# Last layer of a graph network: attention columns inside the weight, denominators inverted on 128 partitions, fusion product in pairs, store in two parts

## What is computed

```python
def gat_conv(x, src, dst, W, att_src, att_dst, bias):   # W: 512 x 4 heads x 64
    h = jnp.einsum('nd,dhc->nhc', x, W)
    a_s = jnp.sum(h * att_src, axis=-1)
    a_d = jnp.sum(h * att_dst, axis=-1)
    e = jax.nn.leaky_relu(a_s[src] + a_d[dst], NEG_SLOPE)
    m = jax.ops.segment_max(e, dst, num_segments=N)
    ex = jnp.exp(e - m[dst])
    denom = jax.ops.segment_sum(ex, dst, num_segments=N)
    alpha = ex / (denom[dst] + 1e-16)
    out = jax.ops.segment_sum(alpha[:, :, None] * h[src], dst, num_segments=N)
    return out.reshape(N, HEADS * C_HEAD) + bias
fwd = gat_conv(x, src, dst, W_f, ...); bwd = gat_conv(x, dst, src, W_b, ...)
fused = jnp.concatenate([fwd, bwd], axis=1) @ W_fuse + b_fuse
mean = jnp.mean(fused, axis=0); var = jnp.mean(jnp.square(fused - mean), axis=0)
out = x + relu((fused - mean) * rsqrt(var + BN_EPS) * bn_gamma + bn_beta)
```

## Time and profile before

| | us |
|---|---|
| median of 3 runs (lowest, highest) | 1034.76 (1033.79, 1034.81) |
| the profiled execution, its own time | 1035.34 |
| its span in the trace | 1033.5 |
| TensorE busy in the span | 882.6 (85%) |
| VectorE busy | 680.3 (66%) |
| POOL busy | 517.6 (50%) |
| ScalarE busy | 454.1 (44%) |
| share of TensorE in the chain that ended last | 61% |

### The profile page before, as it was taken

One profiled execution on the slowest core, in us unless ns is written; L12 is line 12 of the kernel. 1 busy time (PEld: TensorE's weight loads), 2 busy tenths in 40 slices (PEclk: granted clock), 3 DMA queues, 4 the chain that ended last, 5 costly groups with the idle time before them and its releaser, 6 DMA issues.

```text
span 1033.5 us, 18423 instructions
## 1 busy us (share of the span) xinstructions
PE 882.6 (85%) x6852; PEld 767.0 (74%) x6852; DVE 680.3 (66%) x1310; ACT 454.1 (44%) x762; POOL 517.6 (50%) x595
## 2 busy tenths in 40 slices
PE   0789984793899989999989999989999989987785
PEld 0589863672798878798878798878899878854455
DVE  8759957569527677527668437667437578668874
ACT  1277713421347623437523447523347432355652
POOL 6147736124474237674247674246673257356741
PEclk9999998897999999999999999999999999799888
DMA  4000001011430002330002430002330012000001
GB/s 107 22 1 0 0 1 51 11 44 32 101 107 18 1 21 63 103 112 12 1 21 66 115 109 11 1 22 75 110 105 1 1 34 59 11 1 1 0 1 50
DMA packets 45752, 41.32 MB, mean 40 GB/s; under 512 B 4193, under 2 KB 34083, under 8 KB 45690
## 3 DMA queue, kind: packets, MB, share of 16 engines
q1 hardware_dynamic: 43514, 37.19, 12.5%
q10 hardware_dynamic: 2176, 3.32, 1.5%
HBM read 39.08 MB, written 1.28 MB: 39 GB/s over the span
## 4 chain that ended last, share of the span: by engine, by line
PE 61%; DVE 18%; ACT 6%; issue 6%; POOL 4%; DVEq 2%; DMA 1%; SPq 1%; POOLq 0%; ACTq 0%
PE psum L1365 23%; PE psum L1359 16%; PE psum L1457 9%; PE psum L1383 5%; PE psum L730 3%; DVE arena L1767 2%; ACT arena L1243 2%; DVE stats L1911 2%; POOL ringw L1135 1%; PE psum L1408 1%; PE psum L753 1%; DVEq L2005 1%; PE psum L642 1%; DVE hot_dst L2000 1%; DVE x L2103 1%
## 5 line engine op out<-in xcount | busy, mean ns | idle before, releaser
L1365 PE MATMUL psum<-ringw,arena 128*128 128x512 f32 (+2 forms) x558 | 127.5, 387 | 15.5 <-POOL ringw L1135 7.5
L1365 PEld LDWEIGHTS psum<-ringw,arena 128*128 128x128 f32 x558 | 101.4, 213 | 38.0 <-issue 9.1
L1070 POOL TENSOR_SCALAR acc<-acc,rden,flag 128x640 f32<-128x640 f32 x80 | 70.2, 879 | 110.9 <-DVE rden L1763 110.4
L1457 PE MATMUL psum<-ringw,arena 128*128 128x512 f32 x480 | 118.7, 396 | 3.1 <-DVE arena L1775 2.5
L1383 PE MATMUL psum<-ident,acc 128*128 128x128 f32 x560 | 82.5, 280 | 36.3 <-DVE acc L1685 32.3
L1359 PE MATMUL psum<-arena,ringw 128*128 128x320 f32 x768 | 113.3, 309 | 0.0
L1359 PEld LDWEIGHTS psum<-arena,ringw 128*128 128x128 f32 x768 | 112.9, 188 | 0.3
L1135 POOL TENSOR_TENSOR ringw<-raw,ringw 128x512 fp32r<-128x512 f32 x62 | 80.6, 1308 | 56.8 <-ACT ringw L1279 56.8
L1359 PE MATMUL psum<-arena 128*128 128x320 f32 x510 | 95.1, 327 | 14.0 <-issue 7.7
L1457 PEld LDWEIGHTS psum<-ringw,arena 128*128 128x128 f32 x480 | 87.8, 188 | 23.2 <-DVE arena L1775 3.5
L1365 PE MATMUL psum<-arena 128*128 128x256 f32 (+3 forms) x615 | 103.5, 318 | 0.0
(11 more groups left out here) (264 smaller groups left out, 1883.3 us busy)
## 6 DMA issues: line engine op xcount, KB each, us to landing
raw<-in_L_gnn_m_w SPq DMA_DIRECT2D x16, 256.0 KB
xn<-in_L_gnn_m_w SPq DMA_DIRECT2D x16, 256.0 KB
raw<-in_L_gnn_wv SPq DMA_DIRECT2D x8, 256.0 KB
xn<-in_L_gnn_wv SPq DMA_DIRECT2D x8, 256.0 KB
raw<-in_L_gnn_wq SPq DMA_DIRECT2D x8, 256.0 KB
xn<-in_L_gnn_wq SPq DMA_DIRECT2D x8, 256.0 KB
raw<-in_L_gnn_wk SPq DMA_DIRECT2D x8, 256.0 KB
xn<-in_L_gnn_wk SPq DMA_DIRECT2D x8, 256.0 KB
```

The lines of the kernel that those rows point to most:

```text
L1070: g.tensor_scalar(pbuf[:, k % 4, :], pbuf[:, k % 4, :], rden[:, k:k + 1], flag[:, 1, k % NT:k % NT + 1], ALU.mult, ALU.mult).then_inc(pn_u ...
L1365: ins = pe.matmul(to, l, r, start=(i == 0), stop=(i == len(terms) - 1))
L1457: ins = pe.matmul(brow(ROWBLK[f"{name}{t}"]), l, r, start=(pieces[0] + i == 0), stop=(pieces[-1] == KT - 1 and i == len(terms) - 1))
```

## The change

- **Start.** The 16 attention columns join the weight of the b product (`wb`, 272 columns); `own_terms` and `hidden("b", t)` become `hidden_and_own(t)`. VectorE copies the 16 columns tile by tile. All five mask turns and the f product come after three `maxima`, the target rows of the first pair after them.
- **Banks.** A maxima row lies in `source_pair` (banks of `big[1]`, for the second head `big[2]`), branch rows in `target_pair` (`big[0]`, `big[2]` in turn).
- **Order in the turns.** For an even place i the next head's second and first branch stand ahead of the head's first product, for an odd one behind its second, after the target rows. ScalarE's copies move to match.
- **Denominators.** ScalarE copies one row of each. For the first three pairs SP stores it to DRAM, loads it as 128 partitions of 2 x 5, VectorE inverts that, SP stores and loads it back, spread to 64 rows a head. The seventh head is inverted by itself on 64 partitions, the eighth as 128 partitions x 320 columns (`last_sums`).
- **Fusion product.** The first two pairs of column blocks 0 and 1 are multiplied in the last turn, the rest pair by pair. Moments are taken from PSUM; the bias enters the norm's terms.
- **End.** Blocks 0 and 1 are turned, added and stored (256 columns of all tiles), then blocks 2 and 3.
- `DVE_ADDS` has six tiles instead of four.

```diff
-DVE_ADDS = [30, 33, 36, 39]
+DVE_ADDS = [26, 28, 31, 33, 36, 38]
...
+        wide_w = L3H * L3C + 2 * NJ
+        wb = arena2[:, 0:2 * KT * wide_w].rearrange("p (s k c) -> p s k c", s=2, k=KT)
+        AT2 = 2 * KT * wide_w
...
+        den_d = nc.dram_tensor("den_d", [3, 2, NP], F32, kind="Internal").ap()
+        rec_d = nc.dram_tensor("rec_d", [3, 2, NP], F32, kind="Internal").ap()
...
+        def source_pair(i):
+            return big[2 if i == 1 else 1][:, :, 0:HALF]
+
+        def target_pair(i):
+            return big[i % 2 * 2][:, :, 0:HALF]
...
+                    g.wait_ge(share_ld[p], 32)
+                    g.tensor_tensor(comb[:, PAIR[p], :], comb[:, PAIR[p], :], denom[p], ALU.mult).then_inc(comb_up, 1)
...
+                if d == "b":
+                    act.wait_ge(acol_up, t + 1)
...
+                if i == 4 or i == 6:
+                    act.wait_ge(comb_up, p - 1)
+                rows = L3C if i == 6 else 1
+                to = mine if i == 6 else other
...
+                    act.activation(denom[p][to:to + rows, at], pacc[h][other:other + rows, 0:ROW_SPLIT[h]], ACT.Identity,
+                                   bias=tiny[other:other + rows, 0:1]).then_inc(p_read, 1)
...
+            def last_sums():
+
+                act.wait_ge(pa_full, NJ)
+                act.activation(last[L3C:P, :], pacc[0][0:L3C, 0:HALF], ACT.Identity, bias=tiny[0:L3C, 0:1]).then_inc(last_up, 1)
+                act.activation(last[0:L3C, 0:ROW_SPLIT[0] - HALF], pacc[0][0:L3C, HALF:ROW_SPLIT[0]], ACT.Identity,
+                               bias=tiny[0:L3C, 0:1]).then_inc(last_up, 1)
+                act.wait_ge(pb_full, NJ)
+                act.activation(last[0:L3C, ROW_SPLIT[0] - HALF:HALF], pacc[1][0:L3C, 0:ROW_SPLIT[1]], ACT.Identity,
+                               bias=tiny[0:L3C, 0:1]).then_inc(last_up, 1)
+                act.wait_ge(last_rec, 1)
+                act.activation(last_moved[L3C:P, :], last[0:L3C, :], ACT.Copy).then_inc(last_up, 1)
...
-                if st == 1 and i % 2 and i + 1 < NJ:
-                    target_rows((i + 1) // 2)
-                if st == 2 and i + 1 < NJ:
+                if st == 1 and i + 1 < NJ:
+                    if i % 2:
+                        target_rows((i + 1) // 2)
+                    else:
+                        second_branch(i + 1)
+                if st == 2 and i % 2 and i + 1 < NJ:
                     second_branch(i + 1)
-                if st == NT - 1 and i in (4, 6):
-                    comb_high((i - 4) // 2)
+                if st == 0 and i in (5, 7):
+                    comb_high((i - 5) // 2)
+            last_sums()
             comb_high(2)
...
+            def hidden_and_own(t):
+                u = ROW3[f"Hb{t}"]
+                if t < NROW:
+                    free_row(pe, u)
+                else:
+                    pe.wait_ge(h_read, t - NROW + 1)
...
+                row_mm(pe, brow(u)[:, 0:wide_w],
+                       sum([parts(tile_of(yT, k, t), [wb[:, s, k, :] for s in range(2)]) for k in range(KT)], [])).then_inc(h_full, 1)
...
+                if i >= 2:
+                    pe.wait_ge(main_read, MAIN[f"am{max(i - 1, 0) if i > 2 else 0}"] + 1)
...
+                pe.wait_ge(misc_read, MISC[f"vb{i}"] + 1)
...
+            for i in range(EARLY):
+                maxima(i)
             pe.wait_ge(m3_up, NT)
-            mask_turned(0)
-            mask_turned(1)
-            hidden("f", 0)
+            for t in range(NT):
+                mask_turned(t)
+                hidden(t)
             target_rows(0)
-            hidden("f", 1)
             second_branch(0)
             first_branch(0)
...
+                if st == 0 and i % 2 == 0 and i + 1 < NJ:
+                    second_branch(i + 1)
+                    first_branch(i + 1)
...
+                if st == 1 and i % 2 and i + 1 < NJ:
                     target_rows((i + 1) // 2)
-                if st == 1 and i + 1 < NJ:
...
+                    first_branch(i + 1)
+                if st == 2 and i + 4 < NJ:
+                    maxima(i + 4)
+                if n == (NJ - 1) * NT:
+                    fuse(0, range(2))
+                if n == (NJ - 1) * NT + 2:
+                    pe.wait_ge(main_read, MAIN["va6"] + 1)
+                    fuse(1, range(2))
+
+            pe.wait_ge(main_read, len(MAIN))
+            fuse(2, range(2))
+            for o in range(3):
+                fuse(o, range(2, 3))
+            for o in range(3):
                 fuse(o, range(3, 4)).then_inc(f_full, 1)
...
+                dve.reciprocal(dcol[p % 2], dcol[p % 2]).then_inc(rec_up, 1)
...
+            six = comb[0:L3C, PAIR[3], :]
+            dve.wait_ge(p_read, 4 * (NJ - 1))
+            dve.reciprocal(denom[3][0:L3C, :], denom[3][0:L3C, :]).then_inc(rec_up, 1)
+            dve.wait_ge(rec_up, 4)
+            dve.tensor_tensor(six, six, denom[3][0:L3C, :], ALU.mult).then_inc(combd_up, 1)
+            dve.wait_ge(share_ld[2], 32)
+            dve.tensor_tensor(comb[:, PAIR[2], :], comb[:, PAIR[2], :], denom[2], ALU.mult).then_inc(combd_up, 1)
+            dve.wait_ge(last_up, 3)
+            dve.reciprocal(last, last).then_inc(last_rec, 1)
+            dve.wait_ge(last_rec, 1)
+            seven = comb[L3C:P, PAIR[3], :]
+            dve.tensor_tensor(seven[:, 0:HALF], pacc[0][L3C:P, 0:HALF], last[L3C:P, :], ALU.mult).then_inc(combd_up, 1)
+            dve.wait_ge(last_up, 4)
+            cut = ROW_SPLIT[0] - HALF
+            dve.tensor_tensor(seven[:, HALF:ROW_SPLIT[0]], pacc[0][L3C:P, HALF:ROW_SPLIT[0]], last_moved[L3C:P, 0:cut], ALU.mult).then_inc(combd_up, 1)
+            dve.tensor_tensor(seven[:, ROW_SPLIT[0]:NP], pacc[1][L3C:P, 0:ROW_SPLIT[1]], last_moved[L3C:P, cut:HALF], ALU.mult).then_inc(combd_up, 1)
             comb_rest(2)
...
+                dve.wait_ge(f_full, o + 1)
+                for i, n in enumerate((HALF, N - HALF)):
+                    dve.bn_stats(bn3[:, o, i, :], fsum[o][:, i, 0:n]).then_inc(bn_up, 1)
...
+            for p in range(3):
+                sp.wait_ge(p_read, 8 * (p + 1))
+                for h in range(2):
+                    other = (1 - TURN[2 * p + h] % 2) * L3C
+                    sp.dma_start(den_d[p, h:h + 1, :], denom[p][other:other + 1, :]).then_inc(den_st[p], 16)
+                sp.wait_ge(den_st[p], 32)
+                sp.dma_start(dcol[p % 2], den_d[p].rearrange("h (q f) -> q h f", q=P)).then_inc(dcol_ld[p], 16)
+                sp.wait_ge(rec_up, p + 1)
+                sp.dma_start(rec_d[p].rearrange("h (q f) -> q h f", q=P), dcol[p % 2]).then_inc(rec_st[p], 16)
+                sp.wait_ge(rec_st[p], 16)
+                for h in range(2):
+                    mine = TURN[2 * p + h] % 2 * L3C
+                    sp.dma_start(denom[p][mine:mine + L3C, :], rec_d[p, h, :].partition_broadcast(L3C)).then_inc(share_ld[p], 16)
+            sp.wait_ge(y_up, 3)
+            store(sp, 0, 2 * P, False)
+            store(sp, 0, 2 * P, True)
+            sp.wait_ge(y_up, 6)
+            store(sp, 2 * P, 4 * P, False)
+            sp.wait_ge(y_up, 7)
+            store(sp, 2 * P, 4 * P, True)
```

More of the change, by code:

```diff
@@ L102 @@
 MAIN = {n: i for i, n in enumerate(MAIN)}
-MISC = ["mt0", "mt1", "vt0", "vb0", "mt2", "mt3", "mt4"]
+MISC = [f"mt{t}" for t in range(NT)] + ["vt0", "vb0"]
 for _i in range(NJ - 1):
@@ L893, in dve_l3 @@
                     inverse((i - 3) // 2)
[L894 removed]
+                if st == 2 and i in (5, 7):
                     comb_rest((i - 5) // 2)
```

332 lines of the change are left out of this document (155 added, 177 removed).

## The result

The changed kernel takes 1045.8 us (median of 8 runs, 1042.76 to 1047.95), the kernel before on the same chips 1036.75 us (1033.79 to 1040.95): a ratio of 1.0084, 95% interval 1.0062 to 1.0107. It is slower, by about 9 us. The median of before is here 2.0 us above the 1034.76 us that the forecast started from. The profiled execution of the changed kernel takes 1047.22 us, its span is 1045.4 us.

The account below looks back on a forecast made before the run. The prediction took a chain of hand-offs, then TensorE's own order, to bound the turns. Its terms, 0 - 1.0 + 11.4 - 3.15 - 1.4 = +5.9 us, took 1034.76 to 1040.7 us; range 1025 to 1046, own range 1037 to 1044.

Parts of the forecast that it names:

- Start, 0 forecast: Layer start through turn 0: the lead from merged matmuls is spent again, 0 us; -4.3 with the clock kept.
- The fall forecast for this place: Start, at TensorE's wait for the third head's maxima: lower clock for 5 us of work, 2.5 us more.
- Turns without falls, 77.3 forecast: Turns 1 to 7, bound by TensorE's own order, sum to 77.3 us with no fall of the clock.
- Falls, +11.4 forecast: Turns 1 to 6: six falls to the lower clock, mean 1.9 us each, +11.4 us.
- upper bound of 12.6: Turns 1 to 6: most the clock falls were to cost, 6 x 2.1 us; the lower bound was 0.
- turns -1.0: Seven turns: 77.3 us without falls against the old 78.25 us containing three falls, -1.0 us.
- Fusion, -3.15 forecast: From last value product to fusion product's end: 19.1 us becomes 15.95, -3.15 us.
- Rest, -1.4 forecast: Behind the fusion product: moments from PSUM and shorter adds save 1.4 of 11.80 us, between 0 and -3.
- Detour, 0 forecast: Denominators of three pairs through DRAM: transfers covered by the turns, costing nothing.
- the 6.6 us per transfer of the rival: Late denominators' detour: pair 2 delays the last head's chain some 4.2 us, 1044.9 us; chance 0.07.
- the clock stays up: Rival for start and turns: no falls, start -4.3 and falls 0, giving 1025.0 us; chance 0.30.

Follow-up runs that it names:

- e10_start: The changed kernel with the third head's maxima row moved behind the second pair of mask turn and f product at the start: ratio 1.0037 to the kernel before.
- e4_fuses: The changed kernel with the first two pairs' fusion pieces moved from the last turn to behind the last value product: ratio 1.0034 to the kernel before.
- e11_detour2: `e6_all` with the denominators' load of spread sums and store of inverses each made twice in a row: ratio 0.9873 to the kernel before.
- e7_wide: The changed kernel with 2 x 2 overwritten full-width products ahead of the second-branch row of even turns: ratio 0.9991 to the kernel before, turns 83.12 us.
- e6_all: The changed kernel with TensorE's former branch-row order mostly restored and early fusion pieces behind the last product: ratio 0.9883 to the kernel before.
- e8_all_wide: `e6_all` with one overwritten full-width product ahead of the first product of every turn but the last: ratio 0.9848 to the kernel before.

## Why the prediction was right, and where its steps were off

The direction and the mechanism held: 1040.7 forecast from a median of 1034.76, so +5.9 us, against +9 on the same chips. That 1045.8 lies just within the range of 1025 to 1046 is partly luck: it is above the forecast's own 1037 to 1044, and the kernel before was itself 2.0 us slower on these chips.

- **Start, 0 forecast, -1.95 measured, -0.9 by the forecast's own cuts.** Counted from the layer's start, 5.1 us later in this run, the first maximum (893.88) lies at 888.8 and the first product (920.83) at 915.7, where 889 and 916 stood. The wait for the third maxima row was 3.72 us against 3.73:

```profile
897.74 0.89 PE L683 MATMUL psum<-arena 16*128 16x320 f32 x2 [3.72 <-DVE edge_col L849]
```

  The fall forecast for this place came. From the first product to the end of turn 0 it took 7.7 us, where I had 8.3; that and the 0.3 us at the first product are the -0.9. What I missed is that this wait could be avoided by order alone (`e10_start`: -5.0).
- **Turns without falls, 77.3 forecast.** From turns at the full clock: odd 11.17 and 11.48 us (mean 11.33), even 10.63, turn 7 11.56. 3 x 11.33 + 3 x 10.63 + 11.56 = 77.4 us. That the sum agrees to 0.1 us is partly luck: the even turns are 1.2 us longer than worked out, the odd ones 0.8 us and turn 7 0.3 us shorter. The waits themselves were right: 2.7 to 3.0 us in even turns, two of 0.8 us in odd ones.
- **Falls, +11.4 forecast.** 89.97 - 77.4 = 12.5 us, at the upper bound of 12.6. There were six, but in turns 1 to 4, 6 and 7, none in turn 5. The size was off both ways: about 2.0 to 3.2 us for the four long ones, 1.5 us for the two short, where I had 1.9 for all. My mean held 1.6 us for the short fall in turn 7 of the kernel before, and that one cost its turn nothing that shows: 9.78 us, against 9.90 in turn 6 without a fall. TensorE waits 1.30 us for an exponential later in it (to 1000.19), which can hide the slower products.
- **The term "turns -1.0"** was right as a sum and hid the main thing. It set 77.3 us without falls against 78.25 with three. Turns 3 and 5 of the kernel before, at 14.29 and 13.35 us, are 7.6 us longer than two of 10.04. That was what the removed reciprocals could bring. The new order then spent it: turns at the full clock went from 9.9 and 10.04 to 10.63 and 11.33, some 6 us, and the pieces in turn 7 took 2.1 us more and 3.6 with a fall (11.56 and 13.05 against 9.48 without them). I asked whether the reciprocals were worth anything, and pointed to turns 1 and 2, which had none; the turns that had them were the ones to look at. That their removal is what freed turns 3 and 5 is read from the two waits that go back to them; no run removes them alone.
- **Fusion, -3.15 forecast, -2.14 measured.** The third pair's matmuls start 5.4 us after the last product, as worked out (5.55). The sixty matmuls were to take 10.4 us and took 11.46 (1024.09 to 1035.55), since the clock stood at its lower level until 1029.5, 5.4 us of these matmuls; in the kernel before it was 2.9 us (to 1014.3). With 36 matmuls in that wait it did not fall there (`e4_fuses`).
- **Rest, -1.4 forecast, -1.94 measured**, within its bounds.
- **Detour, 0 forecast.** The landing of the spread inverses took 3.2 us:

```profile
z<-rec_d SPq DMA_DIRECT2D x4, 160.0 KB, 3.2
```

  so the 6.6 us per transfer of the rival were far off. In `e11_detour2` the second load, 1.7 us, was over before VectorE came to the inverses, and the second store put the spread load back by 0.7 to 3.2 us; nothing waited for either.

Sum of the terms: -1.95 + 12.8 - 2.1 - 1.9 = +6.8 us against +5.9. The timed runs' +9 has an interval of 6.4 to 11.1 us, which holds the 6.8; whether the rest is chance or lies before the layer stays open. Two readings of the rows were wrong, and nothing in the sum uses them: the matmuls with 16 columns are 60, not 120, and a wait of 2.01 us between heads stands only in turns 1 to 3 (0.58, 2.30, 0.47 and 2.31 us in turns 4 to 7). Of the rivals, "the clock stays up" failed in the changed kernel, and `e7_wide` shows its price there: a ratio of 0.999 with most of the even falls away.

The Trainium skill (TensorE: Matmul & The Clock Gate, HAM oscillation) describes bursts parted by waits that find the clock low each time. In the three even turns the trace agrees: the clock is low from 944.3, 971.5 and 995.3, within the waits of 2.7 to 3.0 us. In turns 1, 3 and 7 it falls with no wait over 1.3 us in the turn, and in turn 5, with the order of turns 1 and 3, it stays at 1.00.

## What to carry to other kernels

An engine that runs in order pays for a wait with everything queued behind it: before moving a row ahead of a product, look at what it waits for on the other engine and how many operations stand before that there. Filling a bank early or starting a product early is worth nothing if the next link of the chain is queued behind it; one change of order here turned +0.8% into -0.7%, and with the fusion pieces moved into -1.2%. Price the clock apart from the waits, by giving TensorE work to do in the wait (a fall costs little where TensorE has to wait behind it anyway), and compare stage by stage when the part before the change wanders by more than the effect.

## What the runs showed of the hardware that was not expected

- More work made the kernel faster: 1.2 us of unused full-width products ahead of the first product of turns 0 to 6 took 4.0 us off the seven turns (72.38 to 68.35), and 2.3 us in three even turns and in turn 0 took 6.9 us off (89.97 to 83.12). Ten matmuls of 8 rows in the same place took nothing off.
- The length of the wait alone does not tell whether the clock falls: not after 2.01 us in the kernel before, but in `e6_all` from 930.8 to 934.3, 1 us behind a wait of 2.01 us that ended at 929.77, and in the changed kernel's turn 3 from 961.3, right behind two waits of 0.8 us between narrow matmuls.
- The same short fall can cost from nothing to 1.7 us: 9.34 us for turn 7 with it (`e8_all_wide`) and without it (`e6_all`), 11.58 against 9.92 us for turn 1.
- An earlier start shifts the falls behind it: the same turn 1 took 12.82 us in the changed kernel and 14.39 us in `e10_start`.
- Identical code before the layer ended anywhere within 10.9 us (867.04 to 877.92), with falls of the clock in different blocks.
